# Reciprocals of the row sums moved from GpSimd to VectorE, and the four value gathers of a batch issued in four successive steps

## Chip, cores and metric

One core of a Trainium2 chip. The time is the device time of the whole program in microseconds (us); its parts are read from one profiled execution.

## What is computed

`x` is 32 sequences of 32 tokens of width 512. A first layer adds to `x` a small product with weights chosen per sequence. The second adds attention with a paged cache: 32 query heads, 8 key/value heads of width 128, and for every sequence 512 cached keys (16 pages of 32) besides its 32 new ones.

```python
scores = jnp.einsum('bqhd,bkhd->bhqk', q, k_all) * SCALE        # q, k normalized and rotated
scores = jnp.where(valid[:, None, None, :], scores, -1e+30)
probs = jax.nn.softmax(scores, axis=-1)
o = jnp.einsum('bhqk,bkhd->bqhd', probs, v_all)
return jnp.einsum('bse,de->bsd', o.reshape(bsz, seqlen, HQ * D), Wo)
```

## The kernel before

The program has two parts. The first, to about 353 us, makes queries, keys and values, splits keys, values and weights into a high and a low half-precision part and stores them. The second is the attention, and the change lies in it. Below, a *batch* is one of the 32 sequences, and a *step* is one of its 8 key/value heads: 4 query heads times 32 tokens are 128 rows on the partitions, against 544 keys. There are NP2 = 256 steps. Each engine runs its own written-out loop over the steps and waits on counters of the others.

In its step i each engine does this:

- TensorE: `transpose_p(i)` (L1396, probabilities of step i to PSUM), in every fourth step `transpose_new` (L1403, the new keys' columns), `scores(i + 3)` (L1385 and L1389; the second half waits for the maximum of step i + 2, which frees the shared PSUM bank), `weigh(i - 2)` (L1421, the value products; at the first head of a batch they wait for the gathered values `d_vs`), in every fourth step `weigh_new` (L1435). Steps 34 to 41, 66 to 73 and so on, eight times in all, also carry a piece of the output projection, `project_out` (L1296).
- VectorE: in every fourth step `ot_lo_of` (L1258), in another `tn_lo` (L1251), both waiting for ScalarE's high part; then `masked_max(i + 3)` (L1237: scores times row scale plus mask to `probs`, and the negated maximum), `t_lo(i)` (L1245, low part of the transposed probabilities), in the first 33 steps `wo_low`.
- ScalarE: the high parts `ot_hi_of` (L950), `tn_hi` (L941), `t_hi(i)` (L934), then `exp(i + 3)` (L927, which also gives `row_sum`), once a batch the mask.
- GpSimd: `norm(i + 2)`: the reciprocal of the row sum (L797, a power of -1, one column) and the scaling of the probabilities by it (L799). Then, in four steps of a batch, one gather of 128 rows of values into a chunk of `vs` (L783, an indirect DMA of about 512 KB) for the next batch.

`vs` has two buffers; the gathers for batch b + 1 wait until the value products of batch b - 1 are done (`t_pv`), and the products of batch b + 1 wait for all four. SyncE's queue loads the queries and 16 key pages of a later batch, once the scores that read the old ones are done, and then the new values. `probs`, `row_sum` and `recip` hold NPR = 6 steps.

Of the kernel before, what the change touches and what calls it, by code (L numbers as in the profile page):

```python
# [12 lines left out]
ALU = mybir.AluOpType  # L13
# [46 lines left out]
def build(nc, x, rows_in, table, l0_w, wq_t, wk_t, wv_t, wo_t, norms_in, kc_t, v_cache, wv,  # L60
# [19 lines left out]
    def sem(name):  # L80
        return persist.enter_context(nc.semaphore(name))
# [25 lines left out]
    minus_one = sb("minus_one", [P, 1])  # L107
# [97 lines left out]
    row_sum = sb("row_sum", [P, NPR])  # L205
    recip = sb("recip", [P, NPR])
# [50 lines left out]
    t_qk, v_max, a_exp = sem("t_qk"), sem("v_max"), sem("a_exp")  # L257
# [1 line left out]
    t_t, a_thi, v_tlo = sem("t_t"), sem("a_thi"), sem("v_tlo")  # L259
    t_tn, a_tnhi, v_tnlo = sem("t_tn"), sem("a_tnhi"), sem("v_tnlo")  # L260
    t_pv, t_pvn = sem("t_pv"), sem("t_pvn")
    p_rec, p_norm, a_mask = sem("p_rec"), sem("p_norm"), sem("a_mask")
    a_wohi, v_wolo, p_wosc, p_wolo = sem("a_wohi"), sem("v_wolo"), sem("p_wosc"), sem("p_wolo")
    a_othi, v_otlo, t_y, v_res = sem("a_othi"), sem("v_otlo"), sem("t_y"), sem("v_res")

# [145 lines left out]
    NP2 = B * HK  # L411
    AHEAD, BEHIND = 3, 2
# [7 lines left out]
    def at(i, place):  # L420

        n, rest = divmod(i - place, HPC)
        return n if rest == 0 and 0 <= n < NHB else None
# [14 lines left out]
    def y_out(i):  # L438

        g, k = divmod(i - (GSTEPS + 2 + YWIN), GSTEPS)  # L440
        return NHALF * g + k // YWIN if 0 <= g < NG and k in (0, YWIN) else None
# [7 lines left out]
    def score_cols(i):  # L449

        return (CH - SEQ * FIRST[0], CH + SEQ * (NPP + 1 - FIRST[0]))[i % 2]

    def rows_of(i):

        b, j = divmod(i, HK)
        g, a = divmod(b, GB)
        return row_scale[:, a, j, g:g + 1]

    def mask_at(i):
        return SEQ * (1 - i % 2)  # L460

    def probs_of(i):
        return probs[:, (i % NPR) // 2, (i % 2) * KEYS:(i % 2 + 1) * KEYS]

    def col(tile, i):
        return tile[:, i % NPR:i % NPR + 1]

    def on_pool(n):
        return n % 4 == 3
# [32 lines left out]
    with persist, nc.Block() as block:  # L502
        @block.sync
        def _(sp):
# [57 lines left out]
            def load_pages(b, first, count):  # L562

                s = b % 2
                at = b * NPP + first
                _, pages = nc.values_load_multi_w_load_instructions(
                    page_ids[0:1, at:at + count], engines=[SP_ENGINE], min_val=0, max_val=PAGES - 1,
                    skip_runtime_bounds_check_because="page_ids is clamped to the pages on the vector engine")
                for pg, page in enumerate(pages):
                    to = BLK + (first + pg) * NHALF * BLK  # L570
                    sp.dma_start(kt[s][:, to:to + NHALF * BLK], k_pages_t[bass.ds(page, 1)].rearrange("a d f -> (a d) f")
                                 ).then_inc(d_kt[s], 16)
# [32 lines left out]
            for u in range(NU):  # L605
# [6 lines left out]
                if LAG < u <= NN + LAG:  # L612
                    un = u - LAG - 1
                    cn, gn = units[un]
                    kind, _, k = chunks[cn]
                    sp.wait_ge(v_rtlo, un + 1)
                    at_k = k if kind == "q" else NHALF - 1 - k
                    dst = (q_t if kind == "q" else k_new_t)[GB * gn:GB * (gn + 1), :, at_k * BLK:(at_k + 1) * BLK]
                    sp.dma_start(dst.rearrange("b d f -> d b f"), stage[un % NST][:].rearrange("p (b f) -> p b f", b=GB)
                                 ).then_inc(d_st[un % NST], 16)  # L620
# [90 lines left out]
        def _(pool):  # L711
# [62 lines left out]
            pool.wait_ge(p_xinv, NG)  # L774
            pool.tensor_tensor(x_norm[:], x_inv[:], minus_one[:].to_broadcast((P, NG)), ALU.pow).then_inc(p_xnorm, 1)

            V_SLOTS = (0, 1, 3, 4)

            def load_v(b, *chunks):
                if b >= 2:  # L780
                    pool.wait_ge(t_pv, HK * (b - 1))
                for c in chunks:
                    pool.indirect_dma_start(vs[b % 2][:, c].rearrange("p j s d -> p (j s d)"), None, v_pages,  # L783
                                            bass.IndirectOffsetOnAxis(
                                                ap=v_row[:, b * NCH + c:b * NCH + c + 1], axis=0)
                                            ).then_inc(d_vs[b % 2], 16)
# [6 lines left out]
            load_v(1, *range(NCH))  # L793

            def norm(i):
                pool.wait_ge(a_exp, i + 1)
                pool.tensor_tensor(col(recip, i), col(row_sum, i), minus_one[:], ALU.pow).then_inc(p_rec, 1)  # L797
                pool.wait_ge(p_rec, i + 1)
                pool.tensor_scalar(probs_of(i), probs_of(i), col(recip, i), 1.0, ALU.mult, ALU.mult).then_inc(p_norm, 1)  # L799

            def wo_low(n):
# [4 lines left out]
                pool.tensor_tensor(wo_lo[:, n, :], wo_nat[n % NWS][:], wo_hi[:, n, :], ALU.subtract).then_inc(p_wolo, 1)  # L806

            norm(0)
            norm(1)
            for i in range(NP2):  # L810
                if i + 2 < NP2:
# [5 lines left out]
                b, rest = divmod(i - 2, HK)  # L817
                if rest in V_SLOTS and 2 <= b + 1 < B:
                    load_v(b + 1, V_SLOTS.index(rest))

# [161 lines left out]
        def _(dve):  # L982
# [246 lines left out]
            def masked_max(i):  # L1229
                dve.wait_ge(t_qk, i + 1)  # L1230
                if i % HK == 0:
                    dve.wait_ge(a_mask, i // HK + 1)
                if i >= NPR:
                    dve.wait_ge(t_t, i - NPR + 1)
                    if i % 2 == 0:
                        dve.wait_ge(t_tn, (i - NPR) // HPC + 1)
                dve.tensor_tensor_reduce(out=probs_of(i), in0=ps_s[:, score_cols(i):score_cols(i) + KEYS],  # L1237
                                         in1=mask[(i // HK) % 2][:, mask_at(i):mask_at(i) + KEYS],
                                         scale=rows_of(i), scalar=3.0e38,
                                         op0=ALU.add, op1=ALU.min,  # L1240
                                         accum_out=col(neg_max, i)).then_inc(v_max, 1)

            def t_lo(i):
                dve.wait_ge(a_thi, i + 1)
                dve.scalar_tensor_tensor(pt_lo[i % NPT][:].rearrange("p c r -> p (c r)"), ps_t[tjob_no["t", i] % NTB][:],  # L1245
                                         P_SCALE, pt_hi[i % NPT][:].rearrange("p c r -> p (c r)"),
                                         ALU.mult, ALU.subtract).then_inc(v_tlo, 1)

            def tn_lo(n):
                dve.wait_ge(a_tnhi, n + 1)  # L1250
                dve.scalar_tensor_tensor(ptn[n % 2][2 * SEQ:4 * SEQ].rearrange("p m r -> p (m r)"),  # L1251
                                         ps_t[tjob_no["tn", n] % NTB][0:2 * SEQ, 0:2 * P], P_SCALE,
                                         ptn[n % 2][0:2 * SEQ].rearrange("p m r -> p (m r)"), ALU.mult, ALU.subtract
                                         ).then_inc(v_tnlo, 1)

            def ot_lo_of(n):
                dve.wait_ge(a_othi, n + 1)
                dve.scalar_tensor_tensor(ot_of(ot_lo, n), ps_o[n % 2][:].rearrange("p (h t) -> p h t", t=SEQ),  # L1258
                                         1.0 / P_SCALE, ot_of(ot_hi, n), ALU.mult, ALU.subtract).then_inc(v_otlo, 1)

            def wo_low(n):
                dve.wait_ge(a_wohi, n + 1)
                dve.scalar_tensor_tensor(wo_lo[:, n, :], wo_nat[n % NWS][:], scale[:, WS:WS + 1], wo_hi[:, n, :],
                                         ALU.mult, ALU.subtract).then_inc(v_wolo, 1)

            def add_residual(w):
                g, half = divmod(w, NHALF)
                dve.wait_ge(t_y, w + 1)
                if w >= 1:
                    dve.wait_ge(v_res, w)  # L1270
                if half == 0:
                    dve.wait_ge(d_res[g % 2], 16 * (g // 2 + 1))
                dve.scalar_tensor_tensor(result[g % 2][:], ps_y(w)[:], y_unscale[:, 0:1], result[g % 2][:],
                                         ALU.mult, ALU.add).then_inc(v_res, 1)

            for i in range(AHEAD):
                masked_max(i)
            for i in range(STEPS):
                if y_out(i) is not None:
                    add_residual(y_out(i))  # L1280
                if at(i, OE) is not None:
                    ot_lo_of(at(i, OE))
                if at(i, TNE) is not None:
                    tn_lo(at(i, TNE))
                if i + AHEAD < NP2:
                    masked_max(i + AHEAD)
                if i < NP2:
                    t_lo(i)
                if 1 <= i <= HQ and not on_pool(i - 1):
                    wo_low(i - 1)  # L1290
# [233 lines left out]
```

## Time and profile before

| | |
|---|---|
| median of 3 runs | 1104.44 us (1103.19 to 1107.31) |
| profiled execution | 1104.1 us, span 1102.3 us |
| TensorE (PE) busy | 1014.0 us, 92% |
| weight loads (PEld) busy | 804.8 us, 73% |
| VectorE (DVE) busy | 757.4 us, 69% |
| ScalarE (ACT) busy | 709.5 us, 64% |
| GpSimd (POOL) busy | 679.5 us, 62% |

Matmuls are pipelined, so busy TensorE is no measure of its limit: how far apart its steps start is. The granted TensorE clock is 0.997 of full speed on the mean. A time such as 709.93 is a place in the span in us. In a row of a timeline, square brackets give how long the engine was idle before, and what released it.

### The profile page before, as it was taken

The numbers are of one execution on the slowest core, as the hardware profiler recorded it, in microseconds if no ns is written. First come the engines' busy times: TensorE is split into PE (matmuls) and PEld (weight loads), VectorE is DVE, ScalarE is ACT, GpSimd is POOL, SyncE is SP. The second block draws the span as 40 slices with busy tenths as digits, with TensorE's granted clock in tenths as the row PEclk, the third lists the DMA queues.
The fourth block names the chain that finished last, engine by engine and source line by source line (L and its number), as shares of the span: only waits on it lengthen the run. The fifth ranks groups of instructions, "written<-read, shape, count | busy, mean of one in ns | idle before, by whom it ended". The sixth has DMA issues, their size and how long they took to land.

```text
span 1102.3 us, 25187 instructions
## 1 busy us (share of the span) xinstructions
PE 1014.0 (92%) x8585; PEld 804.8 (73%) x8585; DVE 757.4 (69%) x1381; ACT 709.5 (64%) x1959; POOL 679.5 (62%) x906
## 2 busy tenths in 40 slices
PE   4899999998999867898999999999999999999998
PEld 2578888886777656677767867877876876886783
DVE  7789999999983777547646746755764773774671
ACT  5899999887743777546635745754753763674570
POOL 5454666568950778747736755864873883784670
PEclk9999999999999999999999999999999999999999
DMA  6799999999988599749847874984974885697440
GB/s 212 237 309 331 342 389 366 329 347 398 357 274 292 163 302 303 253 128 297 278 155 236 268 251 137 294 254 134 313 247 149 283 295 169 220 297 241 154 135 10
DMA packets 203888, 279.72 MB, mean 254 GB/s; under 512 B 26864, under 2 KB 158448, under 8 KB 202224
## 3 DMA queue, kind: packets, MB, share of 16 engines
q1 hardware_dynamic: 185072, 210.86, 57.6%
q0 software_dynamic: 18688, 67.25, 18.5%
q8 instruction: 69, 1.13, 0.4%
q14 instruction: 59, 0.48, 0.1%
HBM read 231.77 MB, written 46.27 MB: 252 GB/s over the span
## 4 chain that ended last, share of the span: by engine, by line
PE 47%; DMA 15%; DVE 12%; issue 10%; POOL 8%; ACT 5%; SPq 3%; DVEq 0%; POOLq 0%; ACTq 0%
PE ps_o L1296 15%; PE ps_proj L1296 14%; DMA vs<-v_pages,v_row 12%; PE ps_o L1421 5%; PE ps_t L1396 3%; POOL probs L799 3%; PE ps_s L1389 3%; PE ps_s L1385 3%; POOL recip L797 2%; DVE probs L1237 2%; POOL vs L783 2%; DMA w_nat<-in_L_cond_Wq 2%; PE ps_rt L1351 2%; DVE c_stage L1160 2%; DVE rot L1132 2%
## 5 line engine op out<-in xcount | busy, mean ns | idle before, releaser
L1237 DVE CUSTOM_DVE_ANT_0 probs<-ps_s,mask,row_scale 128x544 f32<-128x544 f32 x256 | 200.1, 782 | 154.3 <-PE ps_s L1389 125.3
L927 ACT ACTIVATE probs<-probs,neg_max 128x544 f32<-128x544 f32 x256 | 191.3, 747 | 168.9 <-DVE neg_max L1237 144.2
L797 POOL TENSOR_TENSOR recip<-row_sum,minus_one 128x1 f32<-128x1 f32 x256 | 147.9, 578 | 228.3 <-ACT probs L927 220.0
L1421 PE MATMUL ps_o<-pt_hi,vs 128*128 128x128 f16 x2048 | 213.9, 220 | 19.4 <-DMA vs<-v_pages,v_row 17.2
L934 ACT ACTIVATE pt_hi<-ps_t 128x512 f16<-128x512 f32 x256 | 149.1, 582 | 84.0 <-PE ps_t L1396 65.0
L799 POOL TENSOR_SCALAR probs<-probs,recip 128x544 f32<-128x544 f32 x256 | 186.2, 727 | 25.2
L751 POOL TENSOR_TENSOR roped<-rot 128x256 f32<-128x256 f32 x160 | 142.8, 914 | 82.2 <-DVE rot L1124 72.7
L1421 PEld LDWEIGHTS ps_o<-pt_hi,vs 128*128 128x128 f16 x2048 | 167.6, 98 | 28.7 <-DMA vs<-v_pages,v_row 21.9
L1245 DVE SCALAR_TENSOR_TENSOR pt_lo<-ps_t,pt_hi 128x512 f16<-128x512 f32 x256 | 176.0, 688 | 15.3 <-ACT pt_hi L934 15.1
L1421 PE MATMUL ps_o<-pt_lo,vs 128*128 128x128 f16 x1024 | 185.2, 220 | 0.0
L1396 PE MATMUL ps_t<-fixed,probs 128*128 128x128 f32 x1024 | 157.4, 277 | 11.2 <-POOL probs L799 11.2
L1296 PE MATMUL ps_proj<-wt_hi,x0t_hi 128*128 128x512 f32 x384 | 158.6, 413 | 8.1 <-DVE x0t_lo L1025 7.4
L1296 PE MATMUL ps_proj<-wt_hi,x0t_lo 128*128 128x512 f32 x384 | 150.7, 392 | 0.0
L1296 PE MATMUL ps_proj<-wt_lo,x0t_hi 128*128 128x512 f32 x384 | 150.0, 391 | 0.0
L783 POOL DMA_INDIRECT vs<-v_pages,v_row x128 | 134.5, 1051 | 23.5 <-issue 21.5
L1389 PE MATMUL ps_s<-kt,qt 128*128 128x288 f16 (+1 forms) x768 | 126.7, 274 | 21.5 <-DVE neg_max L1237 17.7
L1385 PE MATMUL ps_s<-kt,qt 128*128 128x256 f16 (+1 forms) x768 | 136.8, 287 | 1.6 <-DVE stage L1136 1.6
L1396 PEld LDWEIGHTS ps_t<-fixed,probs 128*128 128x128 f32 x1024 | 112.8, 142 | 27.5 <-POOL probs L799 16.5
L1389 PEld LDWEIGHTS ps_s<-kt,qt 128*128 128x128 f16 x768 | 71.1, 98 | 48.8 <-DVE neg_max L1237 30.6
L1421 PEld LDWEIGHTS ps_o<-pt_lo,vs 128*128 128x128 f16 x1024 | 100.2, 98 | 3.1
L876 ACT ACTIVATE squares<-ps_proj 128x128 bf16<-128x128 f32 x320 | 85.7, 304 | 20.0 <-PE ps_proj L1296 19.7
L1296 PE MATMUL ps_o<-wo_hi,ot_hi 128*128 128x512 f16 x256 | 97.1, 379 | 1.4 <-DVE ot_lo L1258 1.4
(147 smaller groups left out, 1774.0 us busy)
## 6 DMA issues: line engine op xcount, KB each, us to landing
kt<-k_pages_t SPq DMA_DIRECT2D x512, 128.0 KB
c_nat<-in_L_cond_k_cache SPq DMA_DIRECT2D x32, 512.0 KB, 5.9
q_t<-stage SPq DMA_DIRECT2D x64, 256.0 KB, 7.2
c_nat<-in_L_cond_v_cache SPq DMA_DIRECT2D x32, 512.0 KB, 7.0
qt<-q_t SPq DMA_DIRECT2D x32, 512.0 KB
w_nat<-in_L_cond_Wq SPq DMA_DIRECT2D x8, 1024.0 KB, 8.7
k_pages_t<-c_stage SPq DMA_DIRECT2D x16, 512.0 KB, 5.9
c_nat<-in_L_cond_Wo SPq DMA_DIRECT2D x16, 512.0 KB, 7.5
```

The source lines that it names most:

```text
L783: pool.indirect_dma_start(vs[b % 2][:, c].rearrange("p j s d -> p (j s d)"), None, v_pages, bass.IndirectOffsetOnAxis(ap=v_row[:, b * NCH ...
L797: pool.tensor_tensor(col(recip, i), col(row_sum, i), minus_one[:], ALU.pow).then_inc(p_rec, 1)
L799: pool.tensor_scalar(probs_of(i), probs_of(i), col(recip, i), 1.0, ALU.mult, ALU.mult).then_inc(p_norm, 1)
L927: act.activation(pr, pr, ACT.Exp, bias=col(neg_max, i), scale=-1.0, accum_out=col(row_sum, i)).then_inc(a_exp, 1)
L934: act.activation(pt_hi[i % NPT][:].rearrange("p c r -> p (c r)"), ps_t[tjob_no["t", i] % NTB][:], ACT.Copy, scale=P_SCALE).then_inc(a_thi, 1)
L1237: dve.tensor_tensor_reduce(out=probs_of(i), in0=ps_s[:, score_cols(i):score_cols(i) + KEYS], in1=mask[(i // HK) % 2][:, mask_at(i):mask_at ...
L1245: dve.scalar_tensor_tensor(pt_lo[i % NPT][:].rearrange("p c r -> p (c r)"), ps_t[tjob_no["t", i] % NTB][:], P_SCALE, pt_hi[i % NPT][:].rea ...
L1296: ins = pe.matmul(ps, a, b, start=first and n == 0, stop=last and n == len(pairs) - 1)
L1385: pe.matmul(own[0], q[:, a], k[:, b, own[1]:own[2]], start=n2 == 0, stop=n2 == 2)
L1389: ins = pe.matmul(shared[0], q[:, a], k[:, b, shared[1]:shared[2]], start=n2 == 0, stop=n2 == 2)
L1396: ins = pe.transpose(ps_t[tjob_no["t", i] % NTB][:, c * P:(c + 1) * P], probs_of(i)[:, SEQ * (i % 2) + c * P:SEQ * (i % 2) + (c + 1) * P], ...
L1421: ins = pe.matmul(ps_o[n % 2][:, jl * P:(jl + 1) * P], v[:, part, :], p[i % NPT][:, c, :], start=jl == 0 and c == 0 and k == 0, stop=False ...
```

## The change

Two edits. GpSimd's `norm` loses the reciprocal and waits instead for a new counter `v_rec`. VectorE computes the reciprocal of step j in `row_recip(j)`, which waits for the exponential of step j; it stands behind `masked_max(j + 1)` and ahead of `t_lo(j - 2)`. And the gathers that stood in places 0, 1, 3, 4 of a batch's steps on GpSimd stand in places 0, 1, 2, 3.

```diff
-            V_SLOTS = (0, 1, 3, 4)
+            V_SLOTS = (0, 1, 2, 3)
...
             def norm(i):
-                pool.wait_ge(a_exp, i + 1)
-                pool.tensor_tensor(col(recip, i), col(row_sum, i), minus_one[:], ALU.pow).then_inc(p_rec, 1)
-                pool.wait_ge(p_rec, i + 1)
+                pool.wait_ge(v_rec, i + 1)
                 pool.tensor_scalar(probs_of(i), probs_of(i), col(recip, i), 1.0, ALU.mult, ALU.mult).then_inc(p_norm, 1)
...
+            def row_recip(i):
+                dve.wait_ge(a_exp, i + 1)
+                dve.reciprocal(col(recip, i), col(row_sum, i)).then_inc(v_rec, 1)
...
             for i in range(AHEAD):
                 masked_max(i)
+                if i >= 1:
+                    row_recip(i - 1)
...
                 if i + AHEAD < NP2:
                     masked_max(i + AHEAD)
+                if i + AHEAD - 1 < NP2:
+                    row_recip(i + AHEAD - 1)
                 if i < NP2:
                     t_lo(i)
```

## Rows read from the trace of the kernel before

**Rows 1.** Waits between 430 and 1085 us: total, times, longest.
```profile
PEld ps_o L1421 <- DMA vs<-v_pages,v_row: 21.9, 19, 3.1
...
PEld ps_t L1396 <- POOL probs L799: 13.5, 24, 0.9
```

**Rows 2.** Chain that ended last, 640 to 760: start, us, what.
```profile
702.75 7.13 DMA vs<-v_pages,v_row
...
728.22 2.59 PE ps_o L1296 x12
```

**Rows 3.** Timeline of TensorE: start, us, what [idle before it].
```profile
709.93 0.23 PE L1421 MATMUL ps_o<-pt_hi,vs 128*128 128x128 f16 x1 [1.03 <-DMA vs<-v_pages,v_row]
...
716.93 0.61 PE L1396 MATMUL ps_t<-fixed,probs 128*128 128x128 f32 x4
...
720.76 0.61 PE L1396 MATMUL ps_t<-fixed,probs 128*128 128x128 f32 x4
...
723.09 0.66 PE L1396 MATMUL ps_t<-fixed,probs 128*128 128x128 f32 x4 [0.35 <-POOL probs L799]
...
725.39 0.60 PE L1396 MATMUL ps_t<-fixed,probs 128*128 128x128 f32 x4
...
727.37 0.23 PE L1421 MATMUL ps_o<-pt_hi,vs 128*128 128x128 f16 x1 [0.68 <-DMA vs<-v_pages,v_row]
...
816.58 0.23 PE L1421 MATMUL ps_o<-pt_hi,vs 128*128 128x128 f16 x1 [0.61 <-DMA vs<-v_pages,v_row]
```

**Rows 4.** Timeline of VectorE, 712 to 728.
```profile
712.16 0.78 DVE L1237 CUSTOM_DVE_ANT_0 probs<-ps_s,mask,row_scale 128x544 f32<-128x544 f32 x1 [1.19 <-PE ps_s L1389]
...
714.58 0.78 DVE L1237 CUSTOM_DVE_ANT_0 probs<-ps_s,mask,row_scale 128x544 f32<-128x544 f32 x1
...
716.01 0.78 DVE L1237 CUSTOM_DVE_ANT_0 probs<-ps_s,mask,row_scale 128x544 f32<-128x544 f32 x1
...
718.80 0.78 DVE L1237 CUSTOM_DVE_ANT_0 probs<-ps_s,mask,row_scale 128x544 f32<-128x544 f32 x1
...
720.29 0.78 DVE L1237 CUSTOM_DVE_ANT_0 probs<-ps_s,mask,row_scale 128x544 f32<-128x544 f32 x1
...
722.26 0.42 DVE L1251 SCALAR_TENSOR_TENSOR ptn<-ps_t,ptn 64x256 f16<-64x256 f32 x1 [0.57 <-ACT ptn L941]
...
724.48 0.78 DVE L1237 CUSTOM_DVE_ANT_0 probs<-ps_s,mask,row_scale 128x544 f32<-128x544 f32 x1 [0.37 <-PE ps_s L1389]
...
727.38 0.78 DVE L1237 CUSTOM_DVE_ANT_0 probs<-ps_s,mask,row_scale 128x544 f32<-128x544 f32 x1
```

**Rows 5.** Timeline of GpSimd, 717 to 721.
```profile
717.87 1.06 POOL L783 DMA_INDIRECT vs<-v_pages,v_row  x1 [0.17 <-issue]
718.96 0.59 POOL L797 TENSOR_TENSOR recip<-row_sum,minus_one 128x1 f32<-128x1 f32 x1
719.65 0.72 POOL L799 TENSOR_SCALAR probs<-probs,recip 128x544 f32<-128x544 f32 x1
720.54 1.05 POOL L783 DMA_INDIRECT vs<-v_pages,v_row  x1 [0.17 <-issue]
```

**Rows 6.** Busy time by stretch; last three: TensorE clock, DMA share, GB/s.
```profile
677.00:728.00 51.00, 47.60 (x577) 42.70 (x576) 39.24 (x82) 37.07 (x85) 42.44 (x60) 1.00 0.89 295
...
711.00:716.00 5.00, 4.95 (x58) 4.33 (x57) 3.21 (x7) 3.02 (x8) 3.79 (x6) 1.00 0.66 165
```

**Rows 7.** Timeline of VectorE, 311 to 317: its short and its reciprocal instructions.
```profile
311.87 0.15 DVE L1042 TENSOR_REDUCE tops<-abs_sums 128x1 f32<-128x16 f32 x1
311.95 0.41 DVE L1202 TENSOR_TENSOR row_part<-row_part,w_eps 128x256 f32<-128x256 f32 x1
...
315.05 1.75 DVE L1207 RECIPROCAL squares<-squares 128x256 f32<-128x256 f32 x1 [0.87 <-ACT squares L892]
```

**Rows 8.** Timeline of GpSimd beside that reciprocal.
```profile
314.79 0.94 POOL L783 DMA_INDIRECT vs<-v_pages,v_row  x1 [0.30 <-issue]
```

**Rows 9.** Waits between 398 and 476 us.
```profile
PEld ps_t L1396 <- POOL probs L799: 4.7, 6, 0.9
```

More of the change, by code:

```diff
@@ L261, in build @@
     t_pv, t_pvn = sem("t_pv"), sem("t_pvn")
-    p_rec, p_norm, a_mask = sem("p_rec"), sem("p_norm"), sem("a_mask")
+    v_rec, p_norm, a_mask = sem("v_rec"), sem("p_norm"), sem("a_mask")
     a_wohi, v_wolo, p_wosc, p_wolo = sem("a_wohi"), sem("v_wolo"), sem("p_wosc"), sem("p_wolo")
```

## The prediction

> **What bounds the kernel now.** I read the view of waits first. In the attention stretch TensorE idles before two things: the first value product of a batch, which waits for the gathered values (21.9 us over 19 weight loads), and the probability transposes, which wait for GpSimd's normalization (13.5 us over 24) [rows 1]. The stages differ, so an average says little: in one batch of four an output projection adds 8 pieces of 2.59 us to TensorE [rows 2], every other engine catches up, and none of these waits occurs. The change can pay in the other three batches.
>
> Such a batch is the stretch from one first value product to the next: 709.93 to 727.37 is 17.44 us [rows 3]. A whole group of four runs from 727.37 to 816.58, 89.2 us. TensorE alone would need less. Four of its steps, from the transposes at 716.93 to those at 725.39, take 8.46 us, and in them is one wait for GpSimd, ahead of 723.09: 0.35 us on the matrix side, 0.5 on the side of the weight loads (mean 13.5 / 24), which issues first. So 7.94 us are work [rows 1, 3]. That makes 15.9 us a batch; a projection batch is 15.9 + 8 x 2.59 = 36.6; the other three therefore take 89.2 - 36.6 = 52.6, or 17.5 each. So 1.6 us a batch is open.
>
> Now VectorE, which is 69% busy and looks harmless. The starts of its masked maximum are spaced 2.42, 1.43, 2.79, 1.49 from 712.16 to 720.29, together 8.13 us [rows 4]. The 1.43 and 1.49 are the maximum followed at once by the low part: the engine is full. The long ones are full in another way: there ScalarE must finish the exponential and then the high part of the new-key or output tile before VectorE's low part of it can start (the 0.57 us idle at 722.26). The next three spacings, to 727.38, are 7.09 us, with one removable wait, the 0.37 at 724.48 for scores that TensorE's wait had made late (0.34 net of the usual gap). The fourth holds the stall for the values and would be 1.49 without it. VectorE's own chain is then 8.13 + 6.75 + 1.49 = 16.37 us a batch: just above TensorE's 15.9, below today's 17.5. That is where the stall goes: VectorE is late next.
>
> **Gathers.** They are issued behind the normalization of their step. The last two of a batch are out at 717.87 and 720.54: a step that carries one lasts 2.67 us on GpSimd, made of 1.06 gather, 0.59 reciprocal, 0.72 normalization and gaps [rows 5]. The last lands 6.8 (720.54 to 727.37) to 7.1 us after its issue [rows 2, 3, 5]; from the product at 709.93 to its issue are 10.6 us. The change touches this twice. Chunks 2 and 3 go one step earlier, and the reciprocal's 0.59 with its gap leaves the GpSimd step, which comes to about 2.0 us. But the normalization, and so the gather behind it, now also waits for VectorE's next maximum and the reciprocal. The maximum of the batch's first gather step starts at 727.38, 0.7 us behind where the value product would stand without its stall (727.37 - 0.68); then 0.8 for it, 0.15 for the reciprocal with its signals, 0.8 for the normalization, 0.2 to the issue. The first gather thus goes out some 2.7 us after the batch's first value product, later than now. Then come three steps of about 2 us: last issue at 8.7, landing with 7.1 at 15.8 us, against a need at 16.4 to 16.8. So I expect the stall to go, with a margin of only some 0.8 us. The cover is thin because the DMA engines are 89% busy in these batches [rows 6]; the key pages and queries on SP's queue keep their order and triggers, and earlier value transfers can only use what lies idle just behind the batch's start.
>
> **Reciprocal on VectorE.** 256 added, one a step. The profile shows no one-element reciprocal. The nearest rows: an instruction of one result column delays its successor by 0.08 us (311.87 to 311.95), and a reciprocal of 256 columns takes 1.75 us, or at most 7 ns a column [rows 7]. Bounds: 0.08, and 0.18 when nothing overlaps; I take 0.10, near the first, as the neighbours here do not wait for it. Its own wait is for an exponential that ScalarE finished before the maximum now in front of it began or during it, so it costs nothing; queued behind it is the low part, for which TensorE's value products wait two steps later. In the two of four steps with 0.57 us or more idle for ScalarE it is absorbed. In the other two it lengthens VectorE's chain: 4 x 0.10 a batch, 16.37 + 0.40 = 16.8 us. In the projection batches VectorE waits for scores anyway and it is hidden; with that cover gone it would be 0.8 us a batch.
>
> **Normalization later.** The added wait stands ahead of normalization, gather and everything else on GpSimd. From the maximum's start at 718.80: 0.78 + 0.15 + 0.83 ends at 720.56, and the transposes that need it start at 720.76 [rows 3]. So it fits by 0.2; TensorE could be another 0.6 late there before VectorE's chain feels it. The 0.52 us waits of today come from the reciprocal behind a gather, and go.
>
> **First 34 steps** (output weights are split here too): 4.7 us of waits for GpSimd on six transposes [rows 9], of which the loading of these weights on SP's queue, which the change does not touch, may take the place. I take 2 us gain, between 0 and 4.7.
>
> **Sum.** The eight projection batches leave seven stretches of three batches between them: 7 x 3 x (17.5 - 16.8) = 15; rounding inside the unrounded 52.6 - 50.3 gives 16. With the 2 it is 18. Against the profiled execution's own 1104.1 us (span 1102.3) that is 1086, and the median of the runs is 0.3 us above it: **1086 us**. Its own range: reciprocal at 0.08 to 0.18 (plus 2 to minus 7 us), early part 2 us either way, overlap of waits a few: 1078 to 1096.
>
> **Rivals.**
> *The values still come late.* Landing behind the last issue grows from 7.1 to 8 us and more, since the four transfers follow each other closer and run into the key pages. For: 89% DMA use, a first gather that goes out later than now. Against: 0.66 mean use in the 5 us behind a batch's start [rows 6], which the earlier chunks can fill. Every microsecond of landing beyond 8.1 costs 21 us; at 8.7 the batch is back at 17.4 and the time is 1101. Chance 0.15.
> *The reciprocal is held on VectorE, slower than before.* If it had to wait for a running GpSimd instruction of 0.72 us, half of that on average plus 0.10 is 0.46 a step: 16.37 + 1.84 = 18.2 us a batch, 0.7 x 21 = 15 us more: 1118. It decides from 0.28 us a reciprocal on ((17.5 - 16.37) / 4). Against it: the 256-column reciprocal started at 315.05, inside the gather that GpSimd ran from 314.79 for 0.94 us, and was not held to its end [rows 7, 8]. Chance 0.08. The Trainium skill has a rule that would do this: in SBUF - State Buffer, "SBUF: two separate sides", VectorE in a two-port mode and GpSimd exclude each other for a whole instruction. Whether a one-column reciprocal takes that mode no row here shows.
> *Normalization gates TensorE.* The margin of 0.2 fails by more than the 0.6 of play, for instance 0.3 more twice a batch: 21 x 0.6 = 13 us back, 1099. Against: the play itself. Chance 0.09.
> *VectorE does not bind*, because its ScalarE-paced spacings shrink as well: TensorE's 15.9 rules, 7 x 4.9 + 2 = 36 us, 1068. Against: these spacings repeat to 0.1 us. Chance 0.08.
>
> **Chances.** Forecast 0.55, rivals 0.15, 0.08, 0.09, 0.08, something unseen 0.05. The range 1070 to 1102 leaves out the slower rival and most of the fastest. Faster by over 0.5% (5.5 us, about what a measurement can tell from no change): 0.80; within: 0.11; slower: 0.09.
>
> **What would show it.** GpSimd's gather steps at 2.0 instead of 2.67 us; the wait for gathered values near zero; maximum spacings of 1.5 to 1.6 where they were 1.43 and 1.49, unchanged 2.42 and 2.79; batches of 16.8 us; TensorE now waiting for the maximum in small pieces. Wrong if a reciprocal exceeds 0.28 us of VectorE's chain, if the last gather lands over 8 us behind its issue, or if transposes wait for normalization more than today.

## The result

The changed kernel takes 1086.77 us in the median (1086.02 to 1089.67), beside 1104.49 us (1103.19 to 1107.31) for the kernel before. The ratio is 0.9845, with a 95% interval of 0.982 to 0.9871: 1.5% faster. The profiled execution took 1089.67 us (span 1087.9) at a mean TensorE clock of 0.992 instead of 0.997, the slowest of its four runs. 3.3 us of its length arose ahead of the attention, in a part that the change does not touch (there the profiled executions below differ by as much, with the attention starting between 354.2 and 357.9 us).

### The profile after

First the waits in the same stretch as [rows 1], of the changed kernel:

```profile
PEld ps_s L1395 <- DVE neg_max L1235: 24.2, 55, 2.1
...
PEld ps_o L1427 <- DMA vs<-v_pages,v_row: 4.2, 6, 1.0
...
PEld ps_t L1402 <- POOL probs L797: 2.9, 5, 1.7
```

The wait for gathered values is 4.2 us where it was 21.9, the transposes' wait for GpSimd 2.9 where it was 13.5. In their place TensorE's score weights wait more for the maximum: 24.2 us in 55 mostly small pieces, where it was 11.1 us in 23.

In the window of [rows 9], 398 to 476 us, the same wait did not fall. It was 4.7 us in 6:

```profile
PEld ps_t L1402 <- POOL probs L797: 6.0, 8, 1.7
```

VectorE in a batch between projections, as in [rows 4]:

```profile
783.25 0.78 DVE L1235 CUSTOM_DVE_ANT_0 probs<-ps_s,mask,row_scale 128x544 f32<-128x544 f32 x1
...
783.95 0.16 DVE L1243 RECIPROCAL recip<-row_sum 128x1 f32<-128x1 f32 x1
784.02 0.67 DVE L1247 SCALAR_TENSOR_TENSOR pt_lo<-ps_t,pt_hi 128x512 f16<-128x512 f32 x1
784.74 0.78 DVE L1235 CUSTOM_DVE_ANT_0 probs<-ps_s,mask,row_scale 128x544 f32<-128x544 f32 x1
...
786.70 0.42 DVE L1253 SCALAR_TENSOR_TENSOR ptn<-ps_t,ptn 64x256 f16<-64x256 f32 x1 [0.51 <-ACT ptn L939]
787.15 0.79 DVE L1235 CUSTOM_DVE_ANT_0 probs<-ps_s,mask,row_scale 128x544 f32<-128x544 f32 x1
...
787.86 0.16 DVE L1243 RECIPROCAL recip<-row_sum 128x1 f32<-128x1 f32 x1
787.94 0.67 DVE L1247 SCALAR_TENSOR_TENSOR pt_lo<-ps_t,pt_hi 128x512 f16<-128x512 f32 x1
788.58 0.78 DVE L1235 CUSTOM_DVE_ANT_0 probs<-ps_s,mask,row_scale 128x544 f32<-128x544 f32 x1
...
791.83 0.78 DVE L1235 CUSTOM_DVE_ANT_0 probs<-ps_s,mask,row_scale 128x544 f32<-128x544 f32 x1
```

From a maximum at 780.46 on, the starts (L1235) are 2.79, 1.49, 2.42, 1.43, 3.24 and 1.42 us apart, and this repeats in most batches. A batch takes 16.64 us (up to 17.1), where the prediction had read 17.5 and the twelve full batches between projections took 16.9 to 20.6. The reciprocal (L1243) is shown 0.16 us long and starts the low part behind it 0.07 to 0.08 us later. Yet the spacings 1.43 and 1.49 are what they were. One spacing has grown: 3.24 was 2.90.

TensorE beside it: the weights of the second half of the scores, that second half itself, and the first value product of the next batch, which waits for nothing.

```profile
788.00 0.24 PEld L1395 LDWEIGHTS ps_s<-kt,qt 128*128 128x128 f16 x3 [0.33 <-DVE neg_max L1235]
788.00 0.54 PE L1395 MATMUL ps_s<-kt,qt 128*128 128x288 f16 x3
...
790.64 0.22 PE L1427 MATMUL ps_o<-pt_hi,vs 128*128 128x128 f16 x1
```

The maximum of 787.15 lasts 0.78 us, to 787.93. The second half of the scores starts at 788.00 (it needs the bank that this maximum read), lasts 0.54, and the next maximum starts at 788.58. So 1.43 is a loop through TensorE, and the low part, with or without a reciprocal in front of it, lies beside it. The same loop stands in the kernel before, between the maxima of 714.58 and 716.01 [rows 4]:

```profile
715.43 0.24 PEld L1389 LDWEIGHTS ps_s<-kt,qt 128*128 128x128 f16 x3 [0.33 <-DVE neg_max L1237]
```

The 1.49 (783.25 to 784.74) is paced by TensorE too: the second half of the scores ran there from 784.17 for 0.53 us, directly behind other work of TensorE.

GpSimd in the gather steps, as in [rows 5]:

```profile
777.02 1.01 POOL L783 DMA_INDIRECT vs<-v_pages,v_row  x1 [0.15 <-issue]
...
778.97 1.01 POOL L783 DMA_INDIRECT vs<-v_pages,v_row  x1 [0.17 <-issue]
...
780.91 1.01 POOL L783 DMA_INDIRECT vs<-v_pages,v_row  x1 [0.18 <-issue]
781.96 0.73 POOL L797 TENSOR_SCALAR probs<-probs,recip 128x544 f32<-128x544 f32 x1
782.86 1.01 POOL L783 DMA_INDIRECT vs<-v_pages,v_row  x1 [0.17 <-issue]
```

A gather step is 1.95 us where it was 2.67. The batch's first value product is at 774.02, the next batch's at 790.64, 16.62 later. The first gather goes out 3.0 us behind it, the last 8.84. This last one has landed by 790.64, within 7.8 us. Where TensorE did wait, the chain of waits shows how long a last gather took:

```profile
504.61 8.47 DMA vs<-v_pages,v_row
...
538.25 8.22 DMA vs<-v_pages,v_row
...
591.67 8.61 DMA vs<-v_pages,v_row
```

8.2 to 8.6 us, where 6.8 to 7.1 were seen before [rows 2, 5]. But the chain shows only transfers that TensorE waited for, so here it shows the longest ones. The packet records of the two traces show all: for the gathers of batches 8 to 30, the last packet of the last gather ended 6.9 us behind its issue in the median (5.7 to 8.1), and 6.4 us (5.9 to 7.8) in the kernel before. The release, as the chain has it, came 0.4 to 0.7 us after that packet. So the usual transfer became some 0.5 us longer, and a few came to over 8 us.

The whole attention part, from the starts of the maximum (number 0 is the first of the 256):

```
maxima        before us   after us   difference
0                354.52     357.86   +3.3 (start of attention)
0 to 40          113.54     115.36   +1.8
40 to 248        586.92     567.99  -18.9
```

In groups of four batches the third line falls unevenly. From maximum 104 to 232 a group gained 1.9 to 2.4 us, where the prediction's sum has 2.3. The two groups ahead of them, 40 to 104, had been slower before, 91.4 and 92.5 us against 89.0 to 89.2, and gained 4.3 and 5.3.

A loss of this size in the second line has a visible place. ScalarE waited 2.88 us there for a page of the output weights, and TensorE behind it 2.19 us for the low part. One row of ScalarE's timeline, one of TensorE's, and then three stretches (busy time of PE, PEld, DVE, ACT and POOL, granted clock, DMA share, GB/s):

```profile
410.74 0.72 ACT L953 ACTIVATE wo_hi<-wo_nat,scale 128x512 f16<-128x512 f32 x1 [2.88 <-DMA wo_nat<-in_L_cond_Wo]
```

```profile
413.38 0.41 PE L1409 MATMUL ps_t<-fixed,probs 128*64 128x128 f32 x2 [2.19 <-DVE pt_lo L1247]
```

```profile
408.00:415.00 7.00, 3.89 (x44) 3.05 (x41) 2.20 (x6) 4.21 (x8) 2.40 (x3) 0.96 0.92 291
415.00:422.00 7.00, 5.92 (x43) 5.11 (x44) 6.54 (x16) 4.88 (x12) 4.52 (x5) 0.55 0.63 188
760.00:794.00 34.00, 33.41 (x406) 29.78 (x404) 28.14 (x75) 25.33 (x59) 19.73 (x25) 1.00 0.95 313
```

So TensorE was busy for only 3.89 of the 7 us from 408 to 415, and in the 7 us behind them the mean granted clock was 0.55: mostly the lower of the two levels, 1.2 instead of 2.4 GHz. The last row is for the batches seen above: full clock, and the DMA engines 95% busy.

### The profile page after: what moved, and what is told of

It is laid out like the page before. It is cut to its first block, busy times and chain, and to the rows that moved or that the text cites. A ratio compares the mean times of both kernels' runs of the same rounds, so it can differ in the third digit from the quotient of the medians.

```text
span 1087.9 us, 25187 instructions
## 1 busy us (share of the span) xinstructions
PE 1019.6 (94%) x8585; PEld 807.5 (74%) x8585; DVE 773.9 (71%) x1637; ACT 709.5 (65%) x1959; POOL 531.8 (49%) x650
## 4 chain that ended last, share of the span: by engine, by line
PE 58%; DVE 13%; issue 10%; ACT 8%; DMA 7%; POOL 2%; SPq 2%; DVEq 0%; ACTq 0%
PE ps_proj L1302 18%; PE ps_o L1302 15%; PE ps_o L1427 7%; PE ps_t L1402 5%; PE ps_s L1395 4%; DMA vs<-v_pages,v_row 4%; PE ps_s L1391 4%; DVE probs L1235 3%; ACT probs L925 2%; DMA wo_nat<-in_L_cond_Wo 2%; PE ps_rt L1357 2%; DVE c_stage L1158 2%; DVE rot L1130 1%; PE ps_o L1441 1%; POOL probs L797 1%
## 5 line engine op out<-in xcount | busy, mean ns | idle before, releaser
L1235 DVE CUSTOM_DVE_ANT_0 probs<-ps_s,mask,row_scale 128x544 f32<-128x544 f32 x256 | 199.9, 781 | 122.3 <-PE ps_s L1395 119.9
L1247 DVE SCALAR_TENSOR_TENSOR pt_lo<-ps_t,pt_hi 128x512 f16<-128x512 f32 x256 | 172.3, 673 | 21.5 <-ACT pt_hi L932 21.4
L783 POOL DMA_INDIRECT vs<-v_pages,v_row x128 | 131.8, 1029 | 22.7 <-issue 19.7
L1302 PE MATMUL ps_o<-wo_hi,ot_lo 128*128 128x512 f16 x256 | 97.0, 379 | 0.0
```

The lines of the kernel that those rows point to most:

```text
L1302: ins = pe.matmul(ps, a, b, start=first and n == 0, stop=last and n == len(pairs) - 1)
```

## The experiments

Times are medians beside the kernel before on the same chip, ratios with their 95% intervals. "Batch" is the length between projections, from the starts of the maximum.

```
run            us        before     ratio (interval)            batch us
the change     1086.77   1104.49    0.9845 (0.982 to 0.9871)    16.64
slots_only     1094.69   1103.81    0.9922 (0.9895 to 0.9949)   16.7 and 17.2
recip_only     1112.32   1103.81    1.0069 (1.0043 to 1.0095)   16.9 to 21
slots_late     1122.41   1104.13    1.0158 (1.0123 to 1.0193)   17.7 to 21.3
one_more       1090.02   1105.79    0.9857 (0.9828 to 0.9886)   16.64 and 16.8
four_more      1094.79   1105.79    0.9909 (0.988 to 0.9938)    17.13
recip_first    1114.42   1105.79    1.0072 (1.0044 to 1.0099)   18.13
mask_moved     1080.25   1103.81    0.9775 (0.9736 to 0.9813)   16.26 (to 17.7)
lows_last      1095.43   1103.81    0.9925 (0.9898 to 0.9952)   15.8 to 17.2
lows_between   1077.05   1105.79    0.9729 (0.9697 to 0.9761)   15.8 to 19.5
lows_from_42   1073.71   1104.13    0.9727 (0.9702 to 0.9751)   15.8 to 17.0
```

### The two parts by themselves

**slots_only**: the kernel before with

```diff
-            V_SLOTS = (0, 1, 3, 4)
+            V_SLOTS = (0, 1, 2, 3)
```

> The kernel before with the four gathers in successive steps, the reciprocal still on GpSimd. Theory (both parts are needed): the last gather goes out about 8 us behind the first value product instead of 10.6, so the wait for the values goes, but four GpSimd steps of 2.67 us in a row stand against TensorE steps of 2.0, so transposes wait for the normalization instead; batches of about 17.0 us where 17.5 and 16.64 were seen, 1092 to 1098 us. Rival (the slots alone bring the gain): batches of 16.7, 1087 us. Rival (the reciprocal alone brings it): 1104 us.

```profile
PEld ps_t L1396 <- POOL probs L799: 22.5, 37, 1.5
```

```profile
773.24 1.05 POOL L783 DMA_INDIRECT vs<-v_pages,v_row  x1 [0.17 <-issue]
...
775.92 1.05 POOL L783 DMA_INDIRECT vs<-v_pages,v_row  x1 [0.17 <-PE ps_o L1421]
...
778.58 1.06 POOL L783 DMA_INDIRECT vs<-v_pages,v_row  x1 [0.17 <-issue]
```

The wait for values is gone altogether, and the transposes' wait for GpSimd is 22.5 us, more than before. The gather steps are still 2.7 us apart, four in a row now, against about 2 us of a TensorE step. The main theory held: half of the gain, 0.8%. (The profiled execution was the fastest of the six here, the median lies 5 us above it.)

**recip_only**: the changed kernel with the places put back.

```diff
-            V_SLOTS = (0, 1, 2, 3)
+            V_SLOTS = (0, 1, 3, 4)
```

> The changed kernel with the gathers back in places 0, 1, 3, 4. Theory: the normalization waits for the next maximum, so the last gather goes out some 10.4 us behind the first value product and lands 7 us later, at 17.4: the wait for the values stays, batches of 17.3 to 17.6 us, 1100 to 1105 us, although the waits of the transposes for GpSimd are gone. Rival (the reciprocal alone brings the gain): 1087 us, hardly any wait for the values.

Its waits, its last gather of a batch, and that gather in the chain of waits:

```profile
PEld ps_o L1427 <- DMA vs<-v_pages,v_row: 38.4, 20, 3.2
...
PEld ps_t L1402 <- POOL probs L797: 0.6, 1, 0.6
```

```profile
799.39 1.01 POOL L783 DMA_INDIRECT vs<-v_pages,v_row  x1 [0.16 <-issue]
```

```profile
799.39 6.86 DMA vs<-v_pages,v_row
```

The transposes hardly wait any more, but the values cost 38.4 us, more than the 21.9 of the kernel before, and the kernel is slower than it: 1.0069. I had expected no worse than before. The first value product of this batch was at 788.68; its last gather goes out 10.7 us behind it and takes 6.9 us more; before it was 10.6. Other transfers in this run took up to 9.1. Why it is slower than the kernel before and not equal to it stays open; its profile is of the slowest of ten executions.

So the parts are +0.7% and -0.8% alone and -1.5% together. The reciprocal on VectorE makes the gather steps short, but also ties them to the next maximum; that is affordable only one step earlier. The earlier places overload GpSimd as long as it makes the reciprocals.

**slots_late** asks how much room is left: the changed kernel with the places 1, 2, 3, 4.

```diff
-            V_SLOTS = (0, 1, 2, 3)
+            V_SLOTS = (1, 2, 3, 4)
```

> The changed kernel with all four gathers one step later, places 1, 2, 3, 4. It tests how thin the margin of the values is. In the changed kernel the last gather goes out 8.4 us behind the first value product, and where its landing shows in the chain of waits it takes 8.2 to 8.6 us: 16.6 to 17.0, just at the need of 16.64. Theory: one step of 2.0 us later, less what the transfers gain by standing apart, the batch is 17.5 to 18.5 us, a wait for the values at nearly every batch, 1103 to 1120 us. Rival (there is room for a step): below 1092 us.

```profile
PEld ps_o L1427 <- DMA vs<-v_pages,v_row: 41.7, 21, 3.6
```

One step later costs 3.2%, at the upper end. (The 8.4 us in that expectation were a first reading; 8.84 is the figure at the batch shown above.) There is no step of room: the last place is 3, and it fits just so.

### The price of the reciprocal

**one_more** and **four_more** add instructions that nobody reads:

```diff
                 dve.reciprocal(col(recip, i), col(row_sum, i)).then_inc(v_rec, 1)
+                dve.reciprocal(col(spare, i), col(row_sum, i))
```

> The changed kernel with a second reciprocal of the same column into a spare tile right behind the first, read by nobody. It measures the price of one more short instruction on VectorE. In the changed kernel the first left the maximum spacings at 1.43 and 1.49 us, as if it cost nothing: it starts the low part 0.08 us later, which then ends after 0.67 instead of 0.69 us and is followed by the next maximum without its gap. Theory (the gap is used up): the second costs 0.08 us in each of the four full spacings of a batch, batches of 16.9 to 17.0, 1092 to 1095 us. Rival (such instructions hide entirely behind their neighbours): 1087 us.

```diff
                 dve.reciprocal(col(recip, i), col(row_sum, i)).then_inc(v_rec, 1)
+                for k in range(4):
+                    at_k = 4 * (i % NPR) + k
+                    dve.reciprocal(spare[:, at_k:at_k + 1], col(row_sum, i))
```

> The changed kernel with four further reciprocals a step into spare columns, read by nobody. Theory (VectorE with its waits for ScalarE sets the batch): the four full spacings of a batch grow by 4 x 0.08 us, the ones that hold a wait for ScalarE absorb it, the batch goes from 16.64 to about 17.9 us and the time to 1087 + 21 x 1.25 = 1113 us, and the projection batches do not change. Rival (TensorE sets the batch and VectorE has room): 1087 to 1090 us.

VectorE in four_more, behind a maximum that started at 776.47:

```profile
777.17 0.16 DVE L1244 RECIPROCAL recip<-row_sum 128x1 f32<-128x1 f32 x1
777.24 0.33 DVE L1247 RECIPROCAL spare<-row_sum 128x1 f32<-128x1 f32 x4
777.49 0.67 DVE L1251 SCALAR_TENSOR_TENSOR pt_lo<-ps_t,pt_hi 128x512 f16<-128x512 f32 x1
778.42 0.42 DVE L1257 SCALAR_TENSOR_TENSOR ptn<-ps_t,ptn 64x256 f16<-64x256 f32 x1 [0.27 <-ACT ptn L940]
```

With one more the spacing stays 1.43, and 1090.02 us lies above the changed kernel's 1086.77 by less than can be told: it was free as well, so the expectation of 0.08 us a piece was wrong. One spacing of the eight grew from 2.79 to 3.02 in most batches, which I did not follow up; the ratio, 0.9857, can't be told from 0.9845. With four more, 0.25 us together or 0.06 each, the full spacings are 1.61 and the batch 17.13: 0.49 us more, not 1.25. The time is 1094.79 us, between the theory's 1113 and the rival's 1090. The figures fit a lower limit of VectorE's own, 0.78 us from the maximum to the low part with one reciprocal (783.25 to 784.02), 0.06 for each further one, and 0.59 from the low part to the next maximum, about the shortest seen in both runs: 1.37 us with one, 1.43 with two, 1.61 with five. Only the last stands above TensorE's loop of 1.43. The projection steps kept their 4.39 us, as expected.

**recip_first** puts the reciprocal ahead of the maximum, here and likewise in the loop ahead of the steps:

```diff
+                if i + AHEAD - 1 < NP2:
+                    row_recip(i + AHEAD - 1)
                 if i + AHEAD < NP2:
                     masked_max(i + AHEAD)
-                if i + AHEAD - 1 < NP2:
-                    row_recip(i + AHEAD - 1)
```

> The changed kernel with the reciprocal ahead of the next masked maximum instead of behind it, so that the normalization no longer waits for that maximum. Theory: VectorE now waits for the exponential, which ends about 1.0 us behind the previous maximum where the low part ends at 0.7, so each full spacing grows by some 0.3 to 0.4 us, batches of 17.8 to 18.2, 1108 to 1120 us. Rival (the later normalization and gathers cost something in the changed kernel, VectorE nothing): gathers 0.8 us earlier, 1080 to 1087 us.

```profile
780.61 0.69 DVE L1247 SCALAR_TENSOR_TENSOR pt_lo<-ps_t,pt_hi 128x512 f16<-128x512 f32 x1
781.60 0.16 DVE L1243 RECIPROCAL recip<-row_sum 128x1 f32<-128x1 f32 x1 [0.31 <-ACT probs L925]
781.75 0.78 DVE L1235 CUSTOM_DVE_ANT_0 probs<-ps_s,mask,row_scale 128x544 f32<-128x544 f32 x1
```

Between low part and reciprocal VectorE now idles 0.31 us for the exponential, ahead of the maximum for which TensorE and ScalarE wait. The spacings are 1.83 and 1.90, the batch 18.13 us, the time 1114: as the theory said. What made the reciprocal free was its place behind the maximum, where its wait is over and its own time lies beside the scores.

### What sets the batch now

**mask_moved**: ScalarE's mask for the next batch at another place.

```diff
                 if i < NP2:
                     t_hi(i)
+                b, rest = divmod(i, HK)
+                if rest == 2 and 2 <= b + 1 < B:
+                    make_mask(b + 1)
                 if i + AHEAD < NP2:
                     exp(i + AHEAD)
...
-                b, rest = divmod(i, HK)
-                if rest == 0 and 2 <= b + 1 < B:
-                    make_mask(b + 1)
```

> The changed kernel with ScalarE's mask of the next batch computed two steps later and ahead of the exponential, where ScalarE idles 0.97 us for the maximum. Theory (VectorE with its waits for ScalarE sets the batch): the spacing of 3.24 us of the masked maximum falls to 2.79, the batch from 16.64 to 16.2 us, and the time by 21 x 0.45 = 9 us to 1078. Rival (the batch is set by TensorE or by the values): spacings are rearranged, the batch stays at 16.6, 1087 us.

ScalarE in the changed kernel, and then with the mask moved:

```profile
787.98 0.75 ACT L925 ACTIVATE probs<-probs,neg_max 128x544 f32<-128x544 f32 x1 [0.83 <-DVE neg_max L1235]
...
788.73 0.76 ACT L919 ACTIVATE mask<-key_pos,mask_off 128x576 f32<-128x576 f32 x1
789.39 0.57 ACT L932 ACTIVATE pt_hi<-ps_t 128x512 f16<-128x512 f32 x1
789.87 0.73 ACT L925 ACTIVATE probs<-probs,neg_max 128x544 f32<-128x544 f32 x1
```

```profile
785.38 0.59 ACT L932 ACTIVATE pt_hi<-ps_t 128x512 f16<-128x512 f32 x1
785.86 0.77 ACT L919 ACTIVATE mask<-key_pos,mask_off 128x576 f32<-128x576 f32 x1
786.93 0.75 ACT L925 ACTIVATE probs<-probs,neg_max 128x544 f32<-128x544 f32 x1 [0.31 <-DVE neg_max L1235]
```

In the changed kernel the maximum that started at 788.58 was done at 789.36, but its exponential began at 789.87, behind the mask (L919) and the high part that the mask had held up. This is the 3.24. Moved, the mask fills ScalarE's idle time, the spacing is 2.79, the batch 16.26 in half of the cases (others up to 17.7, with waits for the values, 4.8 us in 7), and the time 1080: the theory held to 2 us.

**lows_last**: VectorE no longer stands still for ScalarE.

```diff
-                if at(i, OE) is not None:
-                    ot_lo_of(at(i, OE))
-                if at(i, TNE) is not None:
-                    tn_lo(at(i, TNE))
                 if i + AHEAD < NP2:
                     masked_max(i + AHEAD)
...
                 if i < NP2:
                     t_lo(i)
+                if at(i, OE) is not None:
+                    ot_lo_of(at(i, OE))
+                if at(i, TNE) is not None:
+                    tn_lo(at(i, TNE))
```

> The changed kernel with VectorE's low parts of the new keys and of the output tile moved behind the masked maximum and the low part of the same step, so that they no longer wait for ScalarE. Theory (VectorE's waits for ScalarE set the batch): the spacings 2.42 and 2.79 lose 0.5 and 0.7 us, the batch falls from 16.64 us to TensorE's 15.9, and the time by 21 x 0.7 = 15 us to 1072. Rival (the values land at 15.8 to 16.6 us and bind next): a wait for the values appears, 1078 to 1086. Rival (VectorE does not bind): 1087 us.

A wait of TensorE in a projection, and the busy times (PE, PEld, DVE, ACT, POOL, clock, DMA share, GB/s) over the length of one undisturbed batch:

```profile
741.35 0.39 PE L1302 MATMUL ps_o<-wo_hi,ot_hi 128*128 128x512 f16 x1 [1.48 <-DVE ot_lo L1260]
```

```profile
760.90:776.70 15.80, 15.80 (x198) 14.82 (x196) 13.69 (x37) 12.64 (x30) 9.86 (x12) 1.00 0.88 297
```

Undisturbed batches fell to 15.80 us, the spacings to 2.12, 2.03, 1.81 and 1.94: that is TensorE's own work, busy for all of the 15.80, which the prediction had put at 15.9. Other batches took up to 17.2 us, with waits for key pages (5.7 us in 6) and for values (3.6 us in 8), so the first rival came true beside the theory. The time of 1072 was missed by 23 us: the kernel got slower than the changed one, mostly because a projection piece needs the output tile's low part in the same step: TensorE waited 1.48 us for it here, and two of each projection's spacings are 6.26 instead of 4.3 and 4.45, so some 3.7 us a projection.

**lows_between** has the moved mask and keeps the output tile's low part in front in the projection steps.

```diff
+                first = y_part(i) is not None or i + AHEAD >= NP2
-                if at(i, OE) is not None:
+                if at(i, OE) is not None and first:
                     ot_lo_of(at(i, OE))
-                if at(i, TNE) is not None:
-                    tn_lo(at(i, TNE))
                 if i + AHEAD < NP2:
                     masked_max(i + AHEAD)
...
                     t_lo(i)
+                if at(i, OE) is not None and not first:
+                    ot_lo_of(at(i, OE))
+                if at(i, TNE) is not None:
+                    tn_lo(at(i, TNE))
```

> The kernel with the moved mask, and VectorE's low parts of the new keys and the output tile behind the low part of the step, as in the run with all of them last, but for the output tile in the steps that carry a piece of the projection, where it stays in front. Theory: with all of them last the batches fell to 15.8 us, and 1.87 us were lost at two places of each projection, where TensorE waited for the output tile. So here 15.8 to 15.9 a batch and no loss in the projections: 1080 - 21 x 0.4 = 1072 us. Rival (the values or the key pages bind next, below 16.2 us a batch): their waits appear, 1075 to 1080 us.

The loss in the projections is gone (4.3 and 4.45 again) and batches of 15.80 occur, but others take 16.4 to 19.5, with waits for values (5.5 us in 7) and key pages (6.4 in 3): the rival's mark, 1077 us. **lows_from_42** keeps the old order also in the first 33 steps and for the new keys' low part in all such steps:

```diff
-                first = y_part(i) is not None or i + AHEAD >= NP2
+                first = y_part(i) is not None or i <= HQ or i + AHEAD >= NP2
                 if at(i, OE) is not None and first:
                     ot_lo_of(at(i, OE))
+                if at(i, TNE) is not None and first:
+                    tn_lo(at(i, TNE))
...
-                if at(i, TNE) is not None:
+                if at(i, TNE) is not None and not first:
                     tn_lo(at(i, TNE))
```

> The kernel with the moved mask and the low parts behind the low part of the step, but in the steps up to 32, in those with a piece of the projection and in the last three the old order. In the run before, the first 40 steps took 117.5 us where the moved mask alone took 112.2. Theory: this loss goes, the batches between the projections stay at 15.8 to 16.5 us with some waits for key pages: 1077 - 5 = 1070 to 1074 us. Rival (the first part's 5 us were chance, the transfers bind): 1075 to 1080 us.

```profile
PEld ps_o L1432 <- DMA vs<-v_pages,v_row: 5.5, 10, 1.1
...
PEld ps_t L1407 <- POOL probs L797: 2.2, 3, 1.7
PEld ps_s L1396 <- DMA kt<-k_pages_t: 2.1, 2, 1.2
```

At 1073.71 us, ratio 0.9727, it has the lowest median here, 2.7% below the kernel before, though its interval overlaps lows_between's, and mask_moved's too. The time is the theory's, but the reason I gave is not borne out: the first 40 spacings took 116.6 us in its profile, hardly less than the 117.5 of lows_between and more than the 112.2 of mask_moved. What moves that first part stays open. Between the projections it has ten waits for values and two for key pages, 7.6 us together: the transfers are the next limit.

## Why the prediction came out right, and where its steps were off

Forecast 1086, measured 1086.77. The forecast put 16 us between the projections and 2 in the first 34 steps. Of the first, 18.9 us came, 2.9 more, and this surplus lies in the first two groups of batches. Of the second, nothing that can be told from the clock's changes. That the median was met to 1 us is therefore in part luck; that the two waits go and that the batch falls to just above TensorE's own work was foreseen.

- **The stall for the values goes.** It fell from 21.9 to 4.2 us. The first gather was put at 2.7 us behind the value product (3.0 measured), the last at 8.7 (8.84), a step at 2.0 (1.95). The transfer was the weak term: 7.1 us assumed, some 0.5 us longer in the median by the packets, and 8.2 to 8.6 where TensorE waited. That used up the margin of 0.8 us, and the rival "the values still come late" came true in six places; the prediction's own sign of being wrong, a landing over 8 us behind the last issue, appeared there. slots_late and recip_only show what it costs one step further.
- **The transposes' wait for GpSimd goes.** It fell from 13.5 to 2.9 us, and the spacing that it had lengthened went from 1.77 to 1.43. But the prediction counted this as a gain of 0.34, and it was none: behind it stood ScalarE's mask, and 2.90 became 3.24. The sum of the two, 4.67, did not move until mask_moved.
- **The reciprocal costs 0.10 us in four spacings.** This step failed: it costs nothing that the spacings show. The low part starts 0.07 to 0.08 us later, the price's lower bound, but no spacing grows by it. The prediction read "the maximum followed at once by the low part" as a full engine. The spacing of 1.43 is the maximum, then the second half of the scores through the shared bank, then the maximum; VectorE had 0.06 us to spare even with the reciprocal. one_more, four_more and the TensorE rows show it.
- **VectorE is late next, 16.8 us a batch.** The measured 16.64 lies near it because the two errors cancel: 0.40 us too much for the reciprocal, 0.34 too little for the mask (and 1.42 for 1.49 at the place of the stall). What bound beside TensorE's loop was, in the long spacings, the path of VectorE and ScalarE taking turns: taking the mask out gives 16.26, taking VectorE's waits out 15.80.
- **Normalization has room.** Right between the projections: 5 waits in place of 24, 2.9 us. Not in the first 34 steps, see below.
- **Held reciprocal.** Not seen: its duration is 149 to 164 ns in all 256. But the case that the rival priced, a reciprocal beside a normalization, hardly arises: in 190 of the 256 GpSimd ran nothing at that moment, mostly waiting for this very reciprocal. 57 ran beside the issue of a gather, 8 beside work on the output weights and 1 beside a normalization, and none of these was held either. The rule of the Trainium skill in SBUF - State Buffer, "SBUF: two separate sides", which has VectorE in a two-port mode and GpSimd exclude each other, therefore does not bite a one-column reciprocal in these 66 cases.
- **The first 34 steps** were given 2 us for the waits of six transposes, and this step failed too: these waits did not go, they were 6.0 us in 8 where they were 4.7 in 6, and ScalarE's waits for pages of the output weights rose in the same window from 3.2 to 5.4 us. 1.8 us were lost in the profiled execution, with the clock at 0.55 in it for 7 us. slots_only, at a mean clock of 0.998, took 111.4 us there, 2.2 less than before. The size stays open between these.

## What to carry to other kernels

Two edits that look independent can each be neutral or harmful alone and pay together: here one shortened the steps that the other put in a row, and the other gave back the lateness that the first brought. Cost a handed-over instruction by what its new engine waits for around it, not by its queue being busy: a queue without gaps may still be paced by a loop of exactly that length through another engine. And when a wait is taken away, look at the spacing behind it before counting it: a second delay of the same size can stand right there, as ScalarE's mask did.

## What the runs showed of the hardware

A reciprocal of one column is shown 0.15 to 0.16 us long on VectorE, but further ones start every 0.06 us and the one ahead of a low part delays it by 0.07 to 0.08. The same power of -1 on GpSimd took 0.58 us. The last gather of a batch, 512 KB, took 6.2 to 9.5 us from issue to release where TensorE waited for it in these runs, with the DMA engines 0.89 busy in a stretch of the kernel before and 0.95 in one of the changed kernel. In the changed kernel, with gather steps of 1.95 us, its packets ended some 0.5 us later in the median than in the kernel before; what makes single gathers longer than 8 us is not shown.
